# Weighing the values of a query block in four groups rather than two in a fused scan and attention kernel

## The reference

```python
x = x + scan_block(_gn(x), ...)       # x: (4, 32, 32, 384) f32
x = x + attention(_gn(x), ...)

# attention: 12 heads of 32, L = 1024 positions per image
q, k, v = heads(x @ w_qkv + b_qkv)
q, k = rot(q), rot(k)
attn = einsum('bnqd,bnkd->bnqk', q, k) * 32 ** -0.5
attn = attn + rel_h[..., :, None] + rel_w[..., None, :]
out = einsum('bnqk,bnkd->bnqd', softmax(attn), v)
return out @ w_proj + b_proj
```

## Time and profile before

| | us |
|---|---|
| median of 3 runs | 3247.94 (3243.51 to 3249.18) |
| the profiled execution | 3243.84 |
| its span | 3242.3 |
| TensorE busy | 2795.6 (86%) |
| VectorE busy | 2199.8 (68%) |
| ScalarE busy | 1619.9 (50%) |

### The profile page before, as it was taken

One profiled execution on the slowest core, in us unless ns is written; L12 is line 12 of the kernel. 1 busy time (PEld: TensorE's weight loads), 2 busy tenths in 40 slices (PEclk: granted clock), 3 DMA queues, 4 the chain that ended last, 5 costly groups with the idle time before them and its releaser, 6 DMA issues. The chain is left out here.

```text
span 3242.3 us, 40875 instructions
## 1 busy us (share of the span) xinstructions
PE 2795.6 (86%) x16024; PEld 1414.8 (44%) x16024; DVE 2199.8 (68%) x2149; ACT 1619.9 (50%) x1972; POOL 1339.3 (41%) x624
## 2 busy tenths in 40 slices
PE   6479678878798777787768999999998999989999
PEld 2133233323343332232224565556554665556655
DVE  0398898988989889899862566525664366625665
ACT  2555655555546555464521456424663356515564
POOL 0587877877778777786731100011000100011000
PEclk9799999998999989999887999999999999999999
DMA  2334544454444545444533011020111111020110
GB/s 74 117 141 117 162 147 159 139 140 151 150 161 137 148 144 181 152 139 137 197 107 91 1 34 53 11 63 1 34 53 42 32 34 38 16 72 1 34 53 21
DMA packets 93559, 298.70 MB, mean 92 GB/s; under 512 B 15693, under 2 KB 18521, under 8 KB 93241
## 3 DMA queue, kind: packets, MB, share of 16 engines
q1 hardware_dynamic: 93368, 296.07, 29.4%
HBM read 239.91 MB, written 23.07 MB: 81 GB/s over the span
## 5 line engine op out<-in xcount | busy, mean ns | idle before, releaser
L1617 POOL TENSOR_TENSOR arena<-arena 128x1024 f32<-128x1024 f32 x384 | 901.6, 2357 | 348.3 <-DVE arena L1091 230.9
L1091 DVE TENSOR_TENSOR_SCAN arena<-PS,arena 128x1024 f32<-128x1024 f32 x384 | 879.0, 2289 | 145.0 <-ACT PS L1459 71.6
L586 PE MATMUL PS<-arena,ident 128*128 128x512 f32 x1536 | 772.3, 627 | 14.7 <-ACT arena L1470 12.5
L1459 ACT ACTIVATE PS<-arena,a_inf,a_neg 128x1024 f32<-128x1024 f32 x384 | 463.8, 1208 | 620.3 <-DVE arena L1091 614.3
L1216 DVE CUSTOM_DVE_ANT_1 arena<-PS,arena 128x1024 f32<-128x1024 f32 x384 | 467.4, 1219 | 345.0 <-PE PS L888 345.0
L1543 ACT ACTIVATE arena<-arena,neg_max 128x1024 f32<-128x1024 f32 x384 | 441.1, 1149 | 509.2 <-DVE neg_max L1216 509.2
L577 PE MATMUL PS<-arena,sel 96*128 96x512 bf16 x768 | 241.6, 397 | 325.5 <-DVE arena L1099 321.9
L1099 DVE TENSOR_TENSOR arena<-arena,PS 128x1024 f32<-128x1024 f32 x384 | 460.7, 1200 | 54.0 <-PE PS L577 52.7
L888 PE MATMUL PS<-arena 64*128 64x512 f32 x1536 | 432.5, 641 | 8.8 <-DMA arena<-arena 8.7
L586 PEld LDWEIGHTS PS<-arena,ident 128*128 128x128 f32 x1536 | 306.1, 200 | 279.4 <-issue 225.6
L899 PE MATMUL PS<-ident,arena 128*128 128x128 f32 x3072 | 413.3, 278 | 2.6 <-ACT arena L1543 2.6
(11 more groups left out here) (126 smaller groups left out, 2314.7 us busy)
## 6 DMA issues: line engine op xcount, KB each, us to landing
arena<-b_rows SPq DMA_DIRECT2D x256, 512.0 KB, 3.8
arena<-b_rows SPq DMA_DIRECT2D x256, 256.0 KB, 3.9
arena<-arena SPq DMA_DIRECT2D x192, 128.0 KB, 2.9
arena<-arena SPq DMA_DIRECT2D x120, 64.0 KB, 2.0
normed<-xn SPq DMA_DIRECT2D x5, 1536.0 KB, 6.7
normed<-x_in SPq DMA_DIRECT2D x4, 1536.0 KB, 7.1
residual<-x_in SPq DMA_DIRECT2D x4, 1536.0 KB, 9.3
x<-residual SPq DMA_DIRECT2D x4, 1536.0 KB, 6.5
```

The source lines that it names most:

```text
L586: last = pe.matmul(dst[:, half(h)], lhs, rhs[:, half(h)], start=start, stop=stop, skip_group_check=True)
L1091: dve.tensor_tensor_scan(HS[:, at % 2, ::step], DA[:, ::step], DBU[:, at % R3, ::step], 0.0, ALU.mult, ALU.add).then_inc(scan_done.sem, 1)
L1459: act.activation(DA, DELTA[:, tile % 2, :], ACT.Exp, bias=a_inf[:, col:col + 1], scale=a_neg[:, col:col + 1]).then_inc(da_ready.sem, 1)
L1617: pool.tensor_tensor(DBU[:, at % R3, :], DU[:, tile % 2, :], BSB[:, at % R3, :], ALU.mult).then_inc(dbu_ready.sem, 1)
```

## The change

A block is weighed in four quarters, one in each of steps 4n+5 to 4n+8, in place of halves in steps 4n+5 and 4n+7. A quarter is two parts of keys for four heads. The last quarter of block 22 falls behind the loop. The order of the products within a block, the waits ahead of the first part and the signal behind the last are the same; block 23 is still weighed at once.

```diff
@@ -975,14 +975,15 @@
                         job(g + 1, JOB_AT[g][k])
                     if g + 1 == GROUPS and k in LATE_AT:
                         late(LATE_AT[k])
-                    if s % 2 == 1 and s > HG:
-                        weigh((s - HG - 1) // HG, (s - HG - 1) % HG // 2)
+                    if s > HG:
+                        weigh((s - HG - 1) // HG, (s - HG - 1) % HG, HG)
                     if s + 1 == STEPS * GROUPS:
                         wait_turned_saved(s - 2)
                         project(0, (0, 1))
                         project(1, (0, 1))
                     turn_probs(s)
 
+                weigh(QB * GROUPS - 2, HG - 1, HG)
                 late(("sums", 3))
                 wait_turned_saved(STEPS * GROUPS - 2)
                 project(2, (0, 1))
```

## The result

The change makes the kernel slower: median 3283.57 us against 3245.73, a ratio of 1.0115 with a 95% interval of 1.0101 to 1.0129. The forecast was 3278.2, in a range of 3263 to 3291. As a difference, the forecast was +30.3 us and the measurement is +37.8, so it was 7.5 short. The time itself came only 5.4 above the forecast, because the kernel before had a median 2.2 us lower here than in the three runs that the forecast started from.

What follows compares the result with a forecast made beforehand. TensorE, busy 86% of the span, was taken as the bound. 25.8 + 6.8 + 2.2 - 4.5 = +30.3 us on the profiled 3243.84 gives 3274.1; the median lies 4.1 higher, so 3278.2, range 3263 to 3291.

Steps and rivals of the forecast that it cites:

- L933 and the last quarter: Three L933 groups and the last quarter at each image's end lose a seamless neighbour: 0.14 us each, 2.2 us in all.
- The same products, in more groups: Weighing in attention: 184 more groups, each with 0.14 us of fixed time on TensorE's chain, add 25.8 us.
- The side jobs of the even steps: Jobs in even steps followed by a quarter instead of transposes: 0.09 us more each, 6.8 us in all.
- Waits that take some of it back: Scores' waits for loads of head operands, 8.7 us in 8 waits, absorb part of the added work: -4.5 us.
- What the later end of a block does: Block's finished signal comes one step later; ScalarE's copies still have cover (1.6 and 0.65 us), so it costs nothing.
- A free split: Rival: splitting the weighing costs nothing on TensorE as weight loads run ahead; -1.8 us, 3246; chance 6%.
- A new wait on ScalarE: Rival: later copy of the sums stalls TensorE, at 0.5 us per block adding 46 us, 3324; chance 6%.
- A larger fixed part: Rival: 0.14 + 0.09 us for all 184 groups between other neighbours, +40 us, 3288; an end of the 86% main case.

Runs made afterwards that it cites:

- the whole blocks: Kernel before with each block weighed at once in step 4n+7, in place of two halves: 3241.96 us, ratio 0.9992.
- The control: The kernel before, unchanged, timed against itself: ratio 0.9996 (0.9986 to 1.0006).
- the halves first: Kernel before with the half of the weighing ahead of the step's side job, not behind it: 3243.89 us against 3243.62, ratio 1.0005; second set 0.9994.
- the kernel with the quarters apart: Kernel before with each half split into two quarters in its odd step, one ahead of the transposes, one behind: 3271.91 us against 3247.28, ratio 1.0084.
- The pair of kernels with added work: Kernel before with, in even steps from 6 on, four transposes done twice (3316.77 us) or a quarter weighed once more (3353.51), both against 3247.28.

## Why the prediction was right, and what it lacked

The direction and the mechanism were right: TensorE is the chain, the change adds groups, and no wait gives them back. The measured time lies in the range, 5.4 us above the forecast; 2.2 us of the error are hidden by the lower median of the kernel before, which is luck. By the steps (attention, profile against profile, sums over the groups of the trace):

| step of the prediction | forecast | measured |
|---|---|---|
| 184 groups more | +25.8 | +25.5 |
| side jobs followed by a quarter | +6.8 | +7.2 |
| L933 and the last quarter | +2.2 | +1.5 |
| transposes that no longer follow a job | not counted | +5.0 |
| waits for loads that shrink | -4.5 | -4.9 |
| start of the images | 0 | +2.6 |

**The same products, in more groups.** The 360 quarters ahead of transposes take 0.575 us each, the very value worked out; the fixed part is 0.14 us. Taking it from the difference between the 32 and the 64 records worked because the rest of a group's time grows with its length: 0.575 us for 16 records, 1.01 for 32, and 1.89 for the 64 of the whole blocks.

**The side jobs of the even steps.** This is the step that was short, by a term that the prediction left out. The 0.09 us was read at the job's end, and the reading stopped there. The next row, the scores at 2592.98, would have shown that the transposes behind a job are shorter, too: 0.97 in place of 1.02. An image has 22 such places, 88 in all, at 0.057: 5.0 us. Behind L933 the loss was 0.09, not 0.14. The lesson is on the reading: a group inserted between two others changes the time of both neighbours, and three distances have to be compared, not two.

**Waits that take some of it back.** Held: they went from 8.7 to 3.8 us, where the prediction had 4.2 left. The control's were 7.4 in place of 8.7, so 1 us of this is chance.

**What the later end of a block does.** It was put at nothing, and that held. The cover of the turned copy was given as 0.65 and is 0.66. That this cover is real, and what lies behind it, the whole blocks show: 2.08 + 2.08 us without a weighing, and 0.6 us of stall at once.

**Image starts.** +2.6 us over three images, between an image's first projection and its first rotation (12.3 us each before, 13.2 after). The prediction had no such term. It is the granted clock, 0.86 against 0.79 in the rows above: the lower level lasts longer in all three starts after. That the change does this isn't shown: the halves first, in their second profile, have 13.1 us on average, with the groups of before.

**The rivals.** A free split is out: quarters at 0.575, not 0.44. A new wait on ScalarE is out for the change. A larger fixed part is out between transposes and scores too, by the kernel with the quarters apart. The Trainium skill, "TensorEngine Tiling (Array Packing)", section "Key Properties", says that a change of the tiling mode drains the engine. The pair of kernels with added work agrees that such a change costs time, and gives it a price: 36.7 us over 180 steps, of which 13 were expected for the 88 side jobs. By which means the time goes, a drained array or weights that come late, no run here separates.

## What to carry to other kernels

On a TensorE that hardly idles, count the switches between tile shapes, not only the matmuls: here each added group of 32-column products cost 0.14 us beyond its work, and 0.15 more if it parted two groups of the same tile. Join small groups as long as the light steps that this leaves are still longer than the chain of the other engines, and split only there; put a group of another shape where a switch happens anyway. Spreading work evenly pays only where a wait shows that it is missed. And compare a number between profiles stretch by stretch, with the granted clock of each beside it.

## What the runs showed that I had not expected

- The order of two independent groups within a step is worth 0.149 us each time that it keeps a side job next to transposes of the same tile: 18.5 us in the kernel of the change.
- Fewer groups alone won nothing: 12.7 us less for the weighing, and 19.6 us of stalls on a copy that had 0.5 us of cover.
- The code ahead of attention is the same in all kernels, and in their profiles it ended anywhere from 1782.9 to 1795.4 us. The medians can't tell a gain of 5 us (0.15%) from this, with 11 runs of a kernel against the 27 or 29 of the one before. Much of the scatter goes with the granted clock of the run.
